# The first mixture's expert rows added back inside the next stage's projection

## The reference, cut to what matters

```python
def _L1_ffn_ref(x, ...):                      # mixture: 2 of 8 experts per token
    topk_idx, topk_w = _gate(xf, gate_w, gate_bias)
    ...
    y = jnp.einsum('tkh,tk->th', masked_y, topk_w)        # weighted sum of the two experts' rows
    shared = jax.nn.silu(x @ sw_gate) * (x @ sw_up) @ sw_down
    return y + shared
def _L1_attn_b_ref(x, ...):                   # mixing block
    xn = layer_norm(x, ln1_w, ln1_b)
    q, k, v = (xn @ w.T + b for each of q, k, v)
    q = jax.nn.elu(q) + 1.0; k = jax.nn.elu(k) + 1.0
    ... per token, over heads: kv = k^T v; out = q kv / (q . sum k)
    x = x + attn; x = x + mlp(layer_norm(x))
    return x
x = x + _L1_ffn_ref(_layernorm(x), ...)
x = x + _L1_attn_b_ref(_layernorm(x), ...)
x = x + _L1_ffn_ref(_layernorm(x), ...)
```

## Time and profile before

| | |
|---|---|
| median of the runs | 4086.22 us |
| the profiled execution: its time, its span | 4084.33 us, 4082.4 us |
| busy share of the span: PE, DVE, ACT, POOL | 80%, 66%, 41%, 34% |
| add-back of the first mixture on VectorE | 3101.91 to 3127.34 us |
| projection, first instruction to the next stage | 3128.48 to 3321.25 us |

### The profile page before, as it was taken

The page is one execution under the profiler, slowest core; times in us unless marked ns, Lnnn a source line. Parts: engine busy times, 40 slices in busy tenths (PEclk is TensorE's granted clock), DMA queues, the critical chain, the costliest instruction groups (busy, mean ns, idle before and its releaser), DMA issues. The chain is left out here.

```text
span 4082.4 us, 55633 instructions
## 1 busy us (share of the span) xinstructions
PE 3276.0 (80%) x16440; PEld 1868.5 (46%) x16441; DVE 2677.3 (66%) x5129; ACT 1678.2 (41%) x3247; POOL 1380.2 (34%) x1379
## 2 busy tenths in 40 slices
PE   4877797688659969898898989776794678898885
PEld 1333243233225644444444456554473457666464
DVE  2999899899967757475757667686345556223435
ACT  3655555556415536545564655212031123222222
POOL 2777777677720020201102000352653100001453
PEclk9988898899879979989797999887997889899897
DMA  3555555455520000000000000620244459000146
GB/s 91 134 125 122 122 127 125 108 130 132 133 57 1 0 15 2 2 2 2 2 2 1 2 1 0 176 65 0 85 136 132 108 109 105 21 15 0 56 126 201
DMA packets 370275, 283.15 MB, mean 69 GB/s; under 512 B 214026, under 2 KB 290366, under 8 KB 370016
## 3 DMA queue, kind: packets, MB, share of 16 engines
q1 hardware_dynamic: 356960, 246.43, 25.3%
q0 software_dynamic: 13056, 33.65, 2.4%
HBM read 205.69 MB, written 76.16 MB: 69 GB/s over the span
## 5 line engine op out<-in xcount | busy, mean ns | idle before, releaser
L425 POOL TENSOR_TENSOR mamba_dBu<-mamba_du,mamba_bcs 128x512 f32<-128x512 f32 x512 | 642.9, 1271 | 273.6 <-DMA mamba_bcs<-mamba_bc 213.8
L375 PE MATMUL mamba_banks<-mamba_hc,ident 128*128 128x512 f32 x1024 | 555.3, 664 | 221.3 <-DVE mamba_hc L595 156.2
L548 ACT ACTIVATE mamba_banks<-mamba_delta,mamba_a_neg 128x512 f32<-128x512 f32 x512 | 352.2, 691 | 244.2 <-DVE mamba_hc L595 235.2
L1400 DVE TENSOR_REDUCE attn_mp<-attn_banks 128x1 f32<-128x512 f32 (+3 forms) x768 | 381.9, 550 | 96.9 <-PE attn_banks L1123 54.0
L375 PEld LDWEIGHTS mamba_banks<-mamba_hc,ident 128*128 128x128 f32 x1024 | 194.8, 208 | 544.3 <-DVE mamba_hc L595 310.4
L588 DVE TENSOR_TENSOR_SCAN mamba_banks<-mamba_banks,mamba_dBu 128x512 f32<-128x512 f32 x256 | 312.1, 1219 | 92.4 <-POOL mamba_dBu L425 56.1
L595 DVE TENSOR_TENSOR mamba_hc<-mamba_banks,mamba_bcs 128x512 f32<-128x512 f32 x512 | 343.6, 672 | 21.1 <-PE mamba_banks L375 21.1
L588 DVE TENSOR_TENSOR_SCAN mamba_banks<-mamba_banks,mamba_h_end,mamba_dBu 128x512 f32<-128x512 f32 x256 | 326.9, 1277 | 31.1 <-ACT mamba_banks L548 20.6
L1120 PE MATMUL attn_banks<-attn_kT,attn_qT 96*128 96x512 bf16 (+3 forms) x768 | 273.5, 372 | 10.7 <-ACT attn_kT L1289 5.0
L1136 PE MATMUL attn_banks<-attn_qT,attn_kT 98*128 98x512 bf16 (+3 forms) x768 | 248.6, 339 | 10.2 <-ACT attn_probs L1308 5.3
L1308 ACT ACTIVATE attn_probs<-attn_banks 128x512 f32<-128x512 f32 (+1 forms) x384 | 182.1, 528 | 180.4 <-PE attn_banks L1139 156.0
(11 more groups left out here) (372 smaller groups left out, 6593.4 us busy)
## 6 DMA issues: line engine op xcount, KB each, us to landing
mamba_bcs<-mamba_bc SPq DMA_DIRECT2D x256, 512.0 KB, 5.0
moe_slots_moe<-moe_pad SPq DMA_DIRECT2D x2, 9252.0 KB, 58.1
moe_xg<-moe_slots_moe SPq DMA_DIRECT2D x144, 128.5 KB, 2.1
mix_qkv<-mixA_qkv SPq DMA_DIRECT2D x8, 1536.0 KB, 5.4
moe_xT<-moe_rows SPq DMA_DIRECT2D x16, 512.0 KB, 8.8
moe_rows<-moe_rows SPq DMA_DIRECT2D x16, 512.0 KB, 8.8
mix_qk<-mix_qkv SPq DMA_DIRECT2D x16, 512.0 KB, 7.7
mix_v<-mix_qkv SPq DMA_DIRECT2D x16, 256.0 KB, 7.6
```

Source lines behind the costliest of these rows:

```text
L375: pe.matmul(banks[:, SUMS + k % PAIR, :], c.ident[:, :], hc[:, n % RING, :], start=(st == 0), stop=True, skip_group_check=True).then_inc(s ...
L425: pool.tensor_tensor(dBu[:, n % RING, :], du[:, v, k, :], bcs[:, i_of(n) % 4, 0, :], ALU.mult)\
L548: act.activation(banks[:, n % RING, :], delta[:, v, k, :], ACT.Exp, scale=a_neg[:, k, st:st + 1])\
L1400: dve.tensor_reduce(mp[:, qt // GT, j, qt % GT, at // 512:at // 512 + 1], banks[:, item % SLOTS, 0:size], AX.X, ALU.max).then_inc(sem("rin ...
```

## The change: what it does

- The first mixture ends without the 16 loads and the 64 additions (`for g in range(G if out is not None else 0)`). The second is as it was.
- The projection does it, group by group. SyncE loads a group's two row tiles into `y`, which has two slots; VectorE's `moments(g)` begins with `rejoin(g)`: wait for the loads, then 8 scalar_tensor_tensor instructions as before.
- `qkv` has two slots. The bias addition of a group waits for the store of two groups back.
- z is written between the second and third bias addition, and xn is made on ScalarE (`normalise` of ScalarE, an Identity activation with a scale) rather than on VectorE.
- `low` is gone: the smaller of q/k and 0 and its exponential are both in `expo`. The second copy of the weights, `w0`, is gone too: they are scaled in place, so the scaling waits for the bias projection that reads them.
- The four halves are issued one each behind the stores of groups 2, 3, 4 and 5.
- The weights of the feed-forward layers (`keep_ffn`) are released after their last use, and the mixture's routing weights `w` are kept beyond the first mixture. Both concern memory only.

The core of the diff:

```diff
-                    for g in range(G):
+                    for g in range(G if out is not None else 0):
                         dve.wait_ge(y_back[g], 32)
...
         def walk(engine, one):
 
             one(0, 0, first=True)
-            with engine.Fori(0, (G - 4) // 2) as m:
+            one(1, 1, second=True)
+            with engine.Fori(1, G // 2 - 1) as m:
+                one(m * 2, 0)
                 one(m * 2 + 1, 1)
-                one(m * 2 + 2, 0)
-            one(G - 3, 1)
             one(G - 2, 0, ahead=1)
             one(G - 1, 1, ahead=0)
...
+                def load_y(g, slot):
+                    for i in range(TOP_K):
+                        sp.dma_start(y[:, slot, i, :, :], yd[bass.ds(i * T + g * GN, GN), :].rearrange("(n p) d -> p n d", p=P))\
+                          .then_inc(y_loaded[slot], 16)
+
+                def store(g, slot):
+                    sp.wait_ge(qkv_ready, g * GT + GT)
+                    sp.dma_start(scr[bass.ds(g * GN, GN), :].rearrange("(j p) d -> p j d", p=P), qkv[:, slot, :, :]).then_inc(stored[slot], 16)
+
+                load_y(0, 0)
+                sp.dma_start(w[:, :, :], c.ins["mix_wT"].rearrange("(k p) n -> p k n", p=P)).then_inc(loaded, 16)
                 sp.dma_start(b0[:, :], c.ins["mix_b"].to_broadcast((P, 3 * D))).then_inc(loaded, 16)
                 sp.dma_start(ln[:, :, :], c.ins["mix_ln"].rearrange("(k p) n -> p k n", p=P)).then_inc(loaded, 16)
+                load_y(1, 1)
                 sp.dma_start(rows[2][:, :], c.ins["token_mask"]).then_inc(rows[3], 16)
...
-                for g in range(EARLY + 1):
-                    store(g)
-                sp.wait_ge(stored, 16 * EARLY)
-                sp.wait_ge(cleared, 3)
-                for n in range(SLOTS_M):
-                    load_half(sp, scr, rows, n, n)
-                with sp.Fori(EARLY + 1, G) as g:
-                    store(g)
-                sp.wait_ge(stored, 16 * G)
+                for g in range(G):
+                    if g + 2 < G:
+                        sp.wait_ge(both_added, (g + 1) * GT)
+                        load_y(g + 2, g % 2)
+                    store(g, g % 2)
+                    if g == EARLY:
+                        for slot in range(2):
+                            sp.wait_ge(stored[slot], 16)
+                        sp.wait_ge(cleared, 3)
+                    if EARLY <= g < EARLY + SLOTS_M:
+                        load_half(sp, scr, rows, g - EARLY, g - EARLY)
+                for slot in range(2):
+                    sp.wait_ge(stored[slot], 8 * G)
...
                 norm.power(pool, 0)
+                pool.wait_ge(norm.xn_ready, GT)
                 norm.power(pool, 1)
...
+                def normalise(g):
+                    act.wait_ge(norm.r2_ready, g + 1)
+                    if not (isinstance(g, int) and g == 0):
+                        act.wait_ge(norm.xn_used, g)
+                    for j in range(GT):
+                        act.wait_ge(norm.z_ready, g * GT + j + 1)
+                        act.activation(norm.xn[:, j, :], z[:, bass.ds((g * GT + j) * D, D)], ACT.Identity,
+                                       scale=norm.r2[:, j:j + 1]).then_inc(norm.xn_ready, 1)
...
-                def group(g, slot, first=False, ahead=2):
+                def group(g, slot, first=False, second=False, ahead=2):
                     if ahead >= 1:
                         copy_out(g + 1, 1 - slot, early=first)
-                    exps(g, first)
-
+                    if ahead >= 2:
+                        normalise(g + 2)
+                    exps(g)
+
+                normalise(0)
                 copy_out(0, 0, early=True)
+                normalise(1)
                 walk(act, group)
...
+                def rejoin(g, slot):
+
+                    dve.wait_ge(y_loaded[slot], (g // 2) * 32 + 32 if isinstance(g, int) else (g - slot) * 16 + 32)
+                    tiles = [g * GT + j for j in range(GT)]
+                    for j, t in enumerate(tiles):
+                        dve.scalar_tensor_tensor(c.x_tile(t), y[:, slot, 0, j, :], wy[:, 0, bass.ds(t, 1)], c.x_tile(t), ALU.mult,
+                                                 ALU.add).then_inc(first_added, 1)
+                    for j, t in enumerate(tiles):
+                        dve.wait_ge(first_added, t + 1)
+                        dve.scalar_tensor_tensor(c.x_tile(t), y[:, slot, 1, j, :], wy[:, 1, bass.ds(t, 1)], c.x_tile(t), ALU.mult,
+                                                 ALU.add).then_inc(both_added, 1)
+
+                def moments(g, slot):
+                    rejoin(g, slot)
+                    if not (isinstance(g, int) and g == 0):
+                        dve.wait_ge(norm.r2_ready, g)
+                    dve.wait_ge(both_added, g * GT + GT)
+                    dve.sem_inc(rejoined, 1)
+                    norm.moments(dve, g)
+
+                def take(g, slot, first, second, ahead):
+
+                    if not (first or second):
+                        dve.wait_ge(stored[slot], (g // 2) * 16 if isinstance(g, int) else (g - slot) * 8)
                     if not first:
-                        dve.wait_ge(stored, g * 16)
-                        dve.wait_ge(exp_ready, g * GT)
+                        dve.wait_ge(qkv_ready, g * GT)
                     for j in range(GT):
+                        if j == 2 and ahead >= 2:
+                            normalise(g + 2)
                         dve.wait_ge(qkv_filled, g * GT + j + 1)
-                        dve.tensor_tensor(qkv[:, j, :], qp[:, j % 2, 0:3 * D], bias[:, :], ALU.add).then_inc(qkv_biased, 1)
+                        dve.tensor_tensor(qkv[:, slot, j, :], qp[:, j % 2, 0:3 * D], bias[:, :], ALU.add).then_inc(qkv_biased, 1)
                     for j in range(GT):
...
+                moments(0, 0)
+                normalise(0)
                 dve.wait_ge(loaded, 48)
+                dve.wait_ge(biasp_ready, 1)
                 for k in range(KD):
-                    dve.tensor_scalar(w[:, k, :], w0[:, k, :], ln[:, k, 0:1], None, ALU.mult).then_inc(w_ready, 1)
-                norm.normalise(dve, 0, z_tiles(0), first=True)
-                dve.wait_ge(biasp_ready, 1)
+                    dve.tensor_scalar(w[:, k, :], w[:, k, :], ln[:, k, 0:1], None, ALU.mult).then_inc(w_ready, 1)
                 dve.tensor_tensor(bias[:, :], qp[:, 0, 0:3 * D], b0[:, :], ALU.add).then_inc(bias_ready, 1)
-                norm.moments(dve, 1)
-                norm.normalise(dve, 1, z_tiles(1))
+                moments(1, 1)
+                normalise(1)
...
-                    elu(g)
+                        moments(g + 2, slot)
+                    take(g, slot, first, second, ahead)
+                    elu(g, slot)
```

More of the change, by code:

```diff
@@ L2408, in take, with elu @@
                     for j in range(GT):
                         dve.wait_ge(qkv_biased, g * GT + j + 1)
-                        dve.tensor_scalar(heads(low, j, 2 * MD), heads(qkv, j, HEADW)[:, :, 0:2 * MD], 0.0, None, ALU.min).then_inc(low_ready, 1)
-                def elu(g):
+                        dve.tensor_scalar(heads(expo, j, 2 * MD), heads(qkv[:, slot, :, :], j, HEADW)[:, :, 0:2 * MD], 0.0, None,
+                                          ALU.min).then_inc(low_ready, 1)
+                def elu(g, slot):
@@ L2414, in elu, with normalise @@
                     for j in range(GT):
                         dve.wait_ge(exp_ready, g * GT + j + 1)
-                        qk = heads(qkv, j, HEADW)[:, :, 0:2 * MD]
+                        qk = heads(qkv[:, slot, :, :], j, HEADW)[:, :, 0:2 * MD]
                         dve.scalar_tensor_tensor(qk, qk, 0.0, heads(expo, j, 2 * MD), ALU.max, ALU.add).then_inc(qkv_ready, 1)
-                def z_tiles(g):
-                    return lambda j: z[:, bass.ds((g * GT + j) * D, D)]
-                norm.moments(dve, 0)
+                def normalise(g):
+                    dve.wait_ge(norm.rstd_ready, g + 1)
+                    for j in range(GT):
+                        dve.tensor_scalar(z[:, bass.ds((g * GT + j) * D, D)], c.x_tile(g * GT + j), norm.mv[:, j, 0:1],
+                                          norm.rstd[:, j:j + 1], ALU.subtract, ALU.mult).then_inc(norm.z_ready, 1)
@@ L2428, in _, with group @@
                 dve.tensor_tensor(bias[:, :], qp[:, 0, 0:3 * D], b0[:, :], ALU.add).then_inc(bias_ready, 1)
-                norm.moments(dve, 1)
-                norm.normalise(dve, 1, z_tiles(1))
+                moments(1, 1)
+                normalise(1)
                 dve.wait_ge(bias_ready, 1)
-                def group(g, slot, first=False, ahead=2):
+                def group(g, slot, first=False, second=False, ahead=2):
                     if ahead >= 2:
-                        norm.moments(dve, g + 2)
-                    take(g, first)
-                    if ahead >= 2:
-                        norm.normalise(dve, g + 2, z_tiles(g + 2))
-                    elu(g)
```

(3 more changed lines are left out.)

60 lines of the change are left out of this document (29 added, 31 removed).

## The result

The changed kernel takes 4097.78 us (median of nine runs, 4092.44 to 4099.06), the kernel before, run beside it, 4084.28 us (nine runs, 4082.19 to 4090.31): a ratio of 1.003, 95% interval 1.0019 to 1.004. It is slower by 13.5 us, 0.33%. The forecast was 4087 us. The range 4073 to 4100 held the result, the 4079 to 4095 that carried the chance of 0.58 did not. The profiled execution, the shortest of the nine, took 4092.44 us, span 4090.3 us.

What follows compares the result with a forecast made beforehand. VectorE was taken as main link of a chain per group, with the store in it through the single `qkv`. Start 31.05 us earlier, 45.6 lost to group 5, 13.4 won after: +1.1 us, 4087 us, range 4073 to 4100.

Steps and rivals of the forecast that it cites:

- start S: Start of the projection, forecast at 3097.47 us, 31.05 us earlier than in the kernel before.
- rival C: Third and fourth tile of groups 1 to 5: TensorE stays cold for both, 13 us more, 4100; chance 0.17.
- rival D: SyncE's queue: held issue behind halves and other queue effects beyond 6 us, 4097 or so; chance 0.07.
- Front: End of first mixture: without additions, projection starts a 1.18 us barrier after SyncE's last wait, 31.05 us earlier.
- Prologue: Projection start to group 0's elu end: weights, rows, normalisation and first tiles take 44.8 us.
- Row additions beside the memset: Prologue, additions of group 2 beside GpSimd's memset: no delay taken; a lock on any GpSimd work would cost 4 us.
- Groups 1 to 5: the wait for the rows: Row loads queue behind the previous store: 8.46 us wait, near 14 with a half; 59 us in all.
- The half: Groups 3, 4 and 5: a half in the queue ahead of the rows adds 5.3 us each.
- The cold tile: Groups 1 to 5 after TensorE's idle: one of two tiles at 1.2 GHz, bias to low 9.59 us.
- Rival A: Groups 1 to 5: rows load beside the store, each group gains 2.84 us, 4073; chance 0.14.
- B: Rival for groups 1 to 5: the wait for rows is covered, a group costs 16.3 us, 4018; chance 0.04.
- Groups 6 and 7: Last two groups, without row additions: 22.7 us against 36.1 before, 13.4 us won.

Runs made afterwards that it cites:

- e4_noadd: Kernel before, without the loads and additions of the first mixture's add-back, done nowhere; ratio to before 0.9951.
- e7: e2 with xn made on VectorE, in front of the fourth bias addition, instead of on ScalarE; ratio to the kernel before 0.989.
- e8: Changed kernel, but first mixture adds groups 0 and 1 back, row loads two groups ahead, weights first in queue; ratio to before 0.9861.
- e1: Changed kernel with the rows of group g+3 issued after group g's elu but ahead of its store and half; ratio to before 0.9941.
- e2: Changed kernel with rows issued ahead of the wait for group g's elu, one group earlier than e1; ratio to before 0.9872.
- e3: Changed kernel with one q/k/v buffer, every group waiting for the store of the one before; ratio to the kernel before 1.0074.
- e11: e7 with GpSimd's memsets waiting for xn of group 1; ratio to the kernel before 0.9873.
- e10: e9 with GpSimd's memsets waiting for the bias sum; ratio 0.98, 4083.83 us against 4166.44 us for the kernel before on its chip.
- e9: e8 reordered: row additions and moments between second and third bias addition, transposes between second and third tile, exponentials before xn; ratio to before 0.9816.

## Why the prediction was right, and by how much it was off

Measured against the last indirect DMA, its terms came out so:

| step | forecast | measured | off |
|---|---|---|---|
| last indirect DMA to start S | 3.3 | 10.00 | +6.7 |
| S to the first elu | 44.8 | 44.06 | -0.7 |
| groups 1, 2 | 2 x 27.0 | 27.78, 27.70 | +1.5 |
| groups 3, 4, 5 | 3 x 32.3 | 33.35, 34.17, 33.65 | +4.3 |
| groups 6, 7 | 22.7 | 22.55 | -0.2 |
| last elu to the next stage | 6.5 | 6.44 | -0.1 |

The column sums to 11.5 us, and the forecast's +1.1 becomes the measured 12.6. The mechanism of the groups was right; that the range held the number is in part luck. It reached to 4100 for rival C and counted 4097 to rival D, and neither happened: what lengthened the kernel was the drain, which stands in no rival, and a term of the groups taken 1 us too small, five times.

- *Front.* This is the step that failed: "the barrier takes 1.18 us" was read behind VectorE, where GpSimd had long been drained, and carried to a start behind SyncE's last wait. The barrier's own length is right, 1.1 us; what ends last ahead of it is GpSimd's 10.2 us drain, 6.8 us behind SyncE's wait. e4_noadd shows it alone. The 25 us of additions hid all of it, and I removed the cover without asking what else lay beneath.
- *Prologue.* Right to 0.7 us. ScalarE's xn took 1.71 us for four instructions and not 2.4; the other steps are off by up to 0.5 us each way and cancel.
- *Row additions beside the memset: nothing.* Right: they take 1.67 us for four beside it. The lock on another kind of instruction is real, though (e7, e8). The Trainium skill, "SBUF — State Buffer", Who interferes with whom, has VectorE instructions in a two-port mode (tensor_scalar is one that can enter it) exclude GpSimd's and be excluded, each for a whole instruction, and those with two SBUF inputs contend only with a GpSimd instruction that reads. Both rows agree, 7.06 us for two scalings and 1.67 for four row additions; the mode itself stands in no row.
- *Groups 1 to 5: the wait for the rows.* The mechanism is right; e1 and e2 take it apart. Its size was 9.5 for 8.46 us and 14.8 for 13.8 us, 63.4 us in all for 59. The half is not the cause: it adds 5.26 us (14.78 - 9.52, the means), forecast 5.3. The term that was sized wrong is store and rows, in all five groups. The store of group 0 (1536 KB), with the rows behind it in the queue, lands 6.4 us behind its issue, where before, alone, it took 5.4; the rows land 2.95 us behind it, forecast 2.84.
- *The cold tile.* Right, one of two at 1.2 GHz. Rival C, both cold (some 10 us), has fallen: behind idle times of 14 to 20 us two tiles take 7.0 to 8.2 us, where 5.9 us gave 7.67.
- *Rival A* (loads beside the store) has fallen too: the rows land behind the store and not with it, and with them ahead of the store the wait is 6 us, behind it 9.5. *D,* a held issue behind the halves, has fallen as well: two row loads take 2.79 to 3.43 us to issue behind a half, against 1.68 without, but the sum had 2.84 for them, and the half's whole price is as forecast. *B* is what e2_ahead gives, by moving the loads in one queue: its groups are 18 to 19.4, not 16.3, since TensorE stays cold.
- *Groups 6 and 7.* Right to 0.2 us; e3 shows that the second buffer earns its 15 us there and nowhere else as long as the rows are late.

The chances were too sure of "no change": 0.58 for it, 0.24 for slower, which it was, and both misses, the drain and the store with its rows, lay on the side of slower. The drain should have been a bound: the rows of before said nothing of when GpSimd was ready after its last store, so its cost lay anywhere between nothing and the whole of the cover removed.

## What to carry to other kernels

When a loop takes over work that needs a load, put the load in the queue ahead of anything that waits for the group whose time should cover it; a second buffer doesn't help a transfer that isn't yet issued. Before taking away the last work of a stage, look at what each other engine still has to finish behind it, also what the timeline doesn't count as busy. Then place the moved work where the engine that waits for it has work of its own: with the same additions a group takes 18 to 19 us when they stand at its head, and 14 when they stand between two tiles and TensorE transposes beside them.

## What the runs showed of the chip

- GpSimd's drain at the end of the first mixture lasts 10.17 to 10.19 us in all thirteen kernels, and 9.93 to 10.19 us at the end of the second. The next stage began no earlier than 10.00 us behind the issue of the last indirect DMA. It is not the landing of the rows that ends the drain: SyncE's wait for the last of them is over 2.1 us behind the issue, 6.8 us ahead of the drain's end. What it does wait for wasn't tried.
- While GpSimd's memset of 128x4160 or 128x4096 (3.5 us) runs, VectorE's tensor_scalar from SBUF to SBUF waits: 7.99 us for four instead of 1.14, 7.06 for two instead of 1.15; e11 and e10 show that it is the memset. In e7 and e8 the first instruction stood through both memsets (7.07 and 6.39 us), in before and e9 one got through between them (3.63 and 3.52 us) and the next stood through the second (3.67 and 3.94). Additions with two SBUF inputs, BN_STATS and reads of PSUM kept their length.
- TensorE needed 6.8 to 8.5 us for two tiles behind idle times of 4.83 us (e2) to 20.39 us (after), and 5.4 behind those of 1.6 us at most in e10; the window rows of after show 0.50 for the first tile and 0.98 from the second on. Longer idle times cost no more: 4.94 us gave 8.41 (e2), 20.39 us gave 7.75.
